# Ten unread matmuls in each batch of the second attention, and four stage hand-overs reordered

## The chip, the cores and the metric

One core of a Trainium2 chip. The metric is the device time of one execution in microseconds; the kernel before has three such times, and one more execution was profiled.

## The reference

Two transformer layers on x of shape (8, 256, 256), each a cross attention and a feed-forward, with a residual around every part and a layer norm without weights ahead of it. All is fp32.

```
x = x + mlstm(norm(x), ctx, ctx)       # 8 heads of 32; decay matrix from gates of q, k, v; RMS norm per head
x = x + bitlinear_ffn(norm(x))         # rows rounded to 8 bits, weights to -1, 0, 1; 256 -> 1024 -> 256, gelu
x = x + linear_attention(norm(x), ctx) # phi(q) phi(k)^T with a causal decay, phi = (elu + 1)^5, over its row sum
x = x + moe(norm(x))                   # 8 experts, the 2 best of each row, 256 -> 1024 -> 256, gelu
```

## The kernel before

Rows lie on partitions: 2048 rows are 16 tiles of 128, two tiles to a batch element. The program is a row of blocks, and in each block every engine has its own written-out instruction list; the engines meet by semaphores inside a block, and all of them at its end.

**Gates (L274 to L467).** VectorE normalizes x in four quarters (`normalize`), TensorE transposes them into `qT` and multiplies windows of the gate weights `Z` with the context (L344) and with the queries (`gates`, L350). Tables of decays follow. `keep_running` (L369) issues unread matmuls: products of the identity whose result nobody reads. Eight of them end this block on TensorE.

**mLSTM and first feed-forward (L542 to L1041), one block.** The mLSTM takes 32 steps n, four to a batch (two row tiles by two head groups). TensorE: `state`, `decay`, `scores`, `values`, `far`; ScalarE: exponentials (L772); VectorE: `product`, `joined`, `denominators`, `square_sums`, `refined`, `scaled`, and `row_stats` of batches that are done; GpSimd splits expert weights into a high and a low bf16 part (L208, L210), adds the residual and takes powers (`row_scales`). Around the loop's end stand the first steps of the feed-forward: `centred` and `first_rounded` (ScalarE), `first_scale` and `first_copied` (VectorE), `first_transposes` and `first_product` (TensorE). Each feed-forward step j works on one tile: `hidden` (L974), gelu and sum of squares (ScalarE), `second_root` and `scaled` (GpSimd), `second_scale`, then the second product. TensorE has 4 + 3 unread matmuls in each step (L627). The ternary weights are made from raw loads by ScalarE (`magnitudes`, `rounded_quarter`, `signs`) during the mLSTM.

**Second attention (L1160 on).** Ten steps j of a software pipeline over the eight batches. TensorE's order in step j:

```
queries(j + 1); scores(j); transposed(j - 1); rank(...); attended(j); logits(j - 1)
```

`queries` transposes the normalized rows (L1427), `scores` is phi(k) phi(q) (L1438, L1440), `transposed` (L1449) and `logits` (L1472) serve the gate of the experts, `attended` is the values product (L1457 to L1459). VectorE masks the scores (`weights`, L1644), divides and adds (`attended`, L1648 to L1652), takes statistics, and in steps 3, 5, 6, 7, 8 and 9 chooses experts (`choose`) and computes the rows' places (`slots`, L1684 to L1688). ScalarE makes exponentials and powers of keys and queries and normed rows. GpSimd takes reciprocal roots (`squared_roots`, L1240), the last product of the keys' powers (`keys`, L1218), low parts of rows, and scatters each tile twice into the experts' lists in HBM (`scatter`, L1234). SP loads keys for batch m + 2 once `keys(m)` is done. Every tile's scatter is placed in GpSimd's list by hand: in step j at 4 or above, one tile before `squared_roots` and one behind it; the tiles of the last two batches come after the loop.

At the end TensorE runs 28 unread matmuls, waits for the last scatters' landing, runs ten more, and waits for the rows of the first block (SP, L1193).

**Experts (L1501 on).** 39 blocks of 128 rows: transposes (L1508), first product (L1546), second product (L1559, L1562), and an accumulating scatter into the sum.

## Time and profile before

| | us |
|---|---|
| median of 3 runs | 614.22 (613.63 to 616.29) |
| the profiled execution, its own time | 610.62 |
| its span, first to last instruction | 608.9 |
| mean granted TensorE clock | 0.908 of full speed |
| TensorE busy | 497.8 (82%) |
| VectorE busy | 399.3 (66%) |
| GpSimd busy | 352.3 (58%) |
| ScalarE busy | 303.2 (50%) |

PE is TensorE, PEld its weight loads, DVE VectorE, ACT ScalarE, POOL GpSimd, SP the sync engine; a name with a q (SPq) is an engine's DMA queue or sequencer. Times in rows are us from the span's start. The granted clock is a share of 2.4 GHz: 1.00 is that level and 0.50 the lower one, 1.2 GHz. Shares of busy time are means over stages with different limits.

### The profile page before, as it was taken

The page shows a single profiled execution, that of the slowest core. Times are in us where ns is not written, and L with a number is a line of the kernel's source. Part 1 is how long each engine was busy: PE and PEld are TensorE (multiplying, and loading weights), DVE is VectorE, ACT ScalarE, POOL GpSimd, SP SyncE. Part 2 cuts the span into 40 slices and gives each one's busy share as a digit, 9 for nine tenths or more (in the row PEclk, how much of TensorE's full clock was granted, in tenths as well). Part 3 has the DMA queues.
Part 4 walks back from the last instruction along what each step waited for, and adds up shares of the span by engine and source line. Part 5 has one row for each costly group of instructions (what it writes and reads, how often), then busy time and mean ns, then how long its engine had stood idle before and what let it go on. Part 6 is the DMA issues. An engine that isn't in the chain of part 4 may idle for free. (4 is left out here: it accounts for less than half of the span.)

```text
span 608.9 us, 13847 instructions
## 1 busy us (share of the span) xinstructions
PE 497.8 (82%) x4467; PEld 365.9 (60%) x4467; DVE 399.3 (66%) x1228; ACT 303.2 (50%) x752; POOL 352.3 (58%) x421
## 2 busy tenths in 40 slices
PE   1979999997688878367666658999999999999960
PEld 1845776663355444246556526788878887888740
DVE  3432678998888888456988635566657676666540
ACT  0234575863789988567764313444344434443410
POOL 3509599782888878524686661445555555455531
PEclk9979999997999999857776678999999999999995
DMA  8733633320132232110142264233223323332225
GB/s 280 120 96 121 209 104 114 105 71 18 36 105 92 83 102 73 38 35 23 56 156 87 79 175 133 42 49 54 48 43 54 53 49 53 45 55 30 26 28 154
DMA packets 50614, 50.14 MB, mean 82 GB/s; under 512 B 21584, under 2 KB 40272, under 8 KB 50384
## 3 DMA queue, kind: packets, MB, share of 16 engines
q1 hardware_dynamic: 41168, 36.04, 20.2%
q0 software_dynamic: 7152, 9.36, 9.7%
q10 hardware_dynamic: 2224, 3.86, 2.0%
q8 instruction: 38, 0.62, 0.4%
q14 instruction: 32, 0.26, 0.2%
HBM read 36.46 MB, written 14.87 MB: 84 GB/s over the span
## 5 line engine op out<-in xcount | busy, mean ns | idle before, releaser
L1394 ACT ACTIVATE region<-cps,aux 128x128 f32<-128x128 f32 x312 | 89.3, 368 | 132.3 <-PE cps L1546 132.3
L1285 POOL CAST vaug<-region 128x512 bf16<-128x512 f32 x78 | 49.1, 630 | 107.9 <-ACT region L1394 96.2
L1546 PE MATMUL cps<-aux,w1hi 128*128 128x128 bf16 x1248 | 109.9, 219 | 0.9 <-DVE aux L1754 0.5
L1546 PE MATMUL cps<-aux,w1lo 128*128 128x128 bf16 x624 | 107.5, 217 | 0.0
L1559 PE MATMUL cps<-w2pair,vaug 128*128 x312 | 105.3, 379 | 0.0
L1546 PEld LDWEIGHTS cps<-aux,w1hi 128*128 x1248 | 95.9, 96 | 5.8 <-DVE aux L1754 0.7
L1562 PE MATMUL cps<-w2pair,vaug 128*128 x312 | 78.7, 273 | 0.0
L1291 POOL DMA_INDIRECT y_sum<-aux x39 | 61.0, 1564 | 15.7 <-issue 6.0
L1546 PEld LDWEIGHTS cps<-aux,w1lo 128*128 x624 | 61.5, 98 | 0.0
L1761 DVE TENSOR_TENSOR vaug<-region,vaug 128x512 bf16<-128x512 f32 x78 | 51.2, 697 | 0.1
L1769 DVE TENSOR_TENSOR aux<-cps,wstage 128x256 f32<-128x256 f32 x39 | 16.6, 425 | 52.7 <-PE cps L1559 51.7
L772 ACT ACTIVATE w2pair<-argp,w2pair 128x128 f32<-128x128 f32 x128 | 36.4, 369 | 24.8 <-PE argp L594 24.5
L1559 PEld LDWEIGHTS cps<-w2pair,vaug 128*128 128x128 bf16 x312 | 30.5, 98 | 28.1
L627 PE MATMUL pvp<-aux,identb 128*128 128x512 bf16 x141 | 39.9, 410 | 0.5 <-DVE w2pair L900 0.5
L1234 POOL DMA_INDIRECT row_buf<-region x32 | 34.1, 1064 | 9.2 <-issue 7.5
L210 POOL TENSOR_TENSOR w1lo<-wstage,w1hi 128x512 bf16<-128x512 f32 x32 | 37.2, 1162 | 2.6
L223 POOL TENSOR_TENSOR w2pair<-wstage,w2pair 128x512 bf16<-128x512 f32 x32 | 36.5, 1160 | 0.4 <-ACT w2pair L216 0.4
L617 PE MATMUL pvp<-vaug,w2pair 128*128 128x33 f32 x256 | 34.8, 281 | 1.0 <-DVE w2pair L888 1.0
L1562 PEld LDWEIGHTS cps<-w2pair,vaug 128*128 128x128 bf16 x312 | 30.5, 98 | 7.5
L617 PEld LDWEIGHTS pvp<-vaug,w2pair 128*128 128x128 f32 x256 | 31.2, 192 | 4.8 <-DVE w2pair L888 1.1
L1754 DVE COPY aux<-cps 128x512 bf16<-128x512 bf16 x39 | 16.5, 424 | 25.6 <-PE cps L1508 25.4
L888 DVE SCALAR_TENSOR_TENSOR w2pair<-scp,w2pair 128x512 f32<-128x512 f32 x32 | 21.9, 686 | 16.0 <-PE scp L605 15.5
(274 smaller groups left out, 1113.2 us busy)
## 6 DMA issues: line engine op xcount, KB each, us to landing
wstage<-in_wall SPq DMA_DIRECT2D x64, 256.0 KB, 2.6
aux<-row_buf SPq DMA_DIRECT2D x39, 129.5 KB, 2.1
x_all<-in_x SPq DMA_DIRECT2D x4, 512.0 KB, 8.9
w2pair<-in_ctxT ACTq DMA_DIRECT2D x2, 1024.0 KB, 11.5
vaug<-in_ctx SPq DMA_DIRECT2D x16, 128.0 KB, 4.0
aux<-in_ctxT SPq DMA_DIRECT2D x8, 256.0 KB, 3.0
y_sum<-x_all SPq DMA_DIRECT2D x8, 256.0 KB, 3.2
w2pair<-in_w1T SPq DMA_DIRECT2D x2, 512.0 KB, 4.7
```

The lines of the kernel that those rows point to most:

```text
L210: pool.tensor_tensor(lo, src, hi, ALU.subtract).then_inc(w_split, 1)
L223: pool.tensor_tensor(w2lo[:, n - E, fs], wstage[:, piece(k)].rearrange("p (f n) -> p f n", n=D), w2hi[:, n - E, fs], ALU.subtract).then_in ...
L617: last = pe.matmul(pvp[:, i, cols], pw[:, n % 2, k, :], vaug[:, TB * b + i, cols], start=True, stop=True)
L627: pe.matmul(unread, identb[:, :], w1q[:, 0, 0:512], start=True, stop=True)
L772: last = act.activation(ew[:, n % 2, k, :], argp[:, BANK[n % NU], k * P:(k + 1) * P], ACT.Exp, bias=bT[:, i, at:at + 1])
L1285: pool.tensor_copy(hhi[:, j % 3, n], hf[:, j % 2, n]).then_inc(hi_done, 1)
L1291: pool.indirect_dma_start(y_sum[:, :], bass.IndirectOffsetOnAxis(ap=y_at[:, i % NA:i % NA + 1], axis=0), ys[:, i % NY], None, compute_op=A ...
L1394: last = act.activation(hf[:, j % 2, f * BLK:(f + 1) * BLK], hp[:, j % 2, f, :], ACT.Gelu, bias=b1T[:, bass.ds(e * NF + f, 1)])
L1546: last = pe.matmul(hp[:, j % 2, f, :], w1(cc * NF + f, part), rowsT[:, j % 2, cc, xpart, :], start=(cc == 0 and n == 0), stop=(cc == NC - ...
L1559: return pe.matmul(yp[:, i % 2, 0:2 * D], hhi[:, i % 3, c0:c0 + P], w2(at, 2), start=(f == 0), stop=(f == NF - 1))
L1562: pe.matmul(yp[:, i % 2, 0:D], hlo[:, i % 3, c0:c0 + P], w2(at, 1), start=False, stop=False)
L1761: dve.tensor_tensor(hlo[:, j % 3, n], hf[:, j % 2, n], hhi[:, j % 3, n], ALU.subtract).then_inc(lo_done, 1)
```

## The change

1. **Gates.** The context part of the gate products becomes `context_gates(half)` and stands behind the transposes of quarters 0 and 1. VectorE makes the gate weights behind the first quarter's statistics. The eight unread matmuls at the block's end go; four stand at the head of the next block's list.
2. **mLSTM to feed-forward.** `centred(0)`, `centred(1)` and `first_scale(0)` move into the last steps of the mLSTM, `first_transposes(0)` ahead of the unread matmuls, of which 8 are left of 16. VectorE's order is `first_scale(1)`, `first_copied(0)` directly behind `joined(7)`; `first_copied(1)` and `row_stats(5)` go behind `hidden(0)`. The row scales are made for tiles 0 to 7, 8 to 11 and 12 to 15, the last two in steps 2 and 4.
3. **Scatters.** A table gives the tiles of each step; one more tile in steps 6 and 7, and two instead of four tiles after the loop.
4. **Second attention.** Ten unread matmuls of 512 columns in each batch, each group behind the wait for its bank and ahead of the wait for its input. At the end 44 and 5 instead of 28 and 10.

```diff
-                    keep_running(8)
...
+                        if q < 2:
+                            context_gates(q)
...
-            SCALED_AT = (0, 4, 12, NT)
+            SCALED_AT = (0, 8, 12, NT)
...
+                    for _ in range(4):
+                        pe.matmul(unread, identb[:, :], flat(heads[:, 0:HG, :]), start=True, stop=True)
                     state(0)
...
-                    pe.wait_ge(pv1_read, B)
-                    keep_running(16)
                     pe.wait_ge(exp_done, UN)
                     pe.wait_ge(o_read, B)
                     first_transposes(0)
+                    pe.wait_ge(pv1_read, B)
+                    keep_running(8)
...
+                        if n >= UN - 3 and n < UN - 1:
+                            centred(n - UN + 3)
-                    centred(0)
-                    centred(1)
-                    centred(2)
+                    first_rounded(0)
                     roots(B - 2)
                     squares(B - 1)
-                    first_rounded(0)
                     first_rounded(1)
+                    centred(2)
                     roots(B - 1)
...
-                        if i < 2:
-                            row_scales(i + 1)
+                        if i in (2, 4):
+                            row_scales(i // 2)
...
+                        if n == UN - 1:
+                            first_scale(0)
                     joined(B - 1)
+                    first_scale(1)
+                    first_copied(0)
+                    denominators(B - 1)
                     refined(B - 2)
                     scaled(B - 2)
-                    denominators(B - 1)
                     square_sums(B - 1)
-                    first_scale(0)
-                    row_stats(B - 3)
-                    first_scale(1)
-                    first_copied(0)
-                    first_copied(1)
                     refined(B - 1)
                     scaled(B - 1)
                     dve.wait_ge(bias_in, 32)
                     for j in range(NT + 2):
                         if j < NT:
                             hidden(j)
-                        if j < 2:
-                            row_stats(B - 2 + j)
+                        if j == 0:
+                            first_copied(1)
                         if j + 2 < NT:
                             first_scale(j + 2)
+                        if j < 3:
+                            row_stats(B - 3 + j)
...
+            SCATTERED = {4: ((0,), (1,)), 5: ((2,), (3,)), 6: ((4,), (5, 6)), 7: ((7,), (8, 9)), 8: ((10,), (11,)), 9: ((12, 13), ())}
...
-                    for b in range(ENDS - 4, B):
-                        scatter(b, 0)
-                        scatter(b, 1)
+                    for i in range(NT - TB, NT):
+                        scatter(i)
...
                     def queries(b):
-                        pe.wait_ge(xc_ready, b + 1)
                         if b:
                             pe.wait_ge(eq_ready, b)
+                        keep_running(5)
+                        pe.wait_ge(xc_ready, b + 1)
...
                     def transposed(b):
-                        pe.wait_ge(xn_ready, b + 1)
                         if b:
                             pe.wait_ge(xt_ready, b)
+                        keep_running(2, 4)
+                        pe.wait_ge(xn_ready, b + 1)
...
                     def attended(b):
-                        pe.wait_ge(w_ready, b + 1)
                         if b:
                             pe.wait_ge(x_done, b)
+                        keep_running(3, 2)
+                        pe.wait_ge(w_ready, b + 1)
...
-                    def keep_running(k):
+                    def keep_running(k, bank=0):
                         for _ in range(k):
-                            pe.matmul(banks[:, 0], identb[:, :], w1hi[:, 0, 0:512], start=True, stop=True)
+                            pe.matmul(banks[:, bank], identb[:, :], w1hi[:, 0, 0:512], start=True, stop=True)
...
-                    keep_running(28)
+                    keep_running(44)
                     pe.wait_ge(moved[(B - 1) % NPK], 16 * 2 * TB * (B // NPK))
-                    keep_running(10)
+                    keep_running(5)
```

## Rows read from the trace of the kernel before

**Rows 1.** Chain that ended last: start us, us, what.
```profile
365.70 4.45 PE cps L1478 x10
```

**Rows 2.** Busy us of each engine by stretch (x instructions), granted clock, DMA.
```profile
137.20:150.20 13.00, 10.48 (x38) 4.84 (x38) 10.21 (x37) 3.87 (x8) 2.56 (x2) 0.74 0.07 21
150.20:250.90 100.70, 78.52 (x463) 45.62 (x463) 81.60 (x217) 81.60 (x124) 82.03 (x101) 0.98 0.23 74
250.90:352.30 101.40, 62.72 (x320) 51.89 (x321) 75.14 (x268) 57.67 (x114) 58.63 (x63) 0.67 0.23 74
```

**Rows 3.** Timeline, gates to mLSTM: start us, us, engine line, [idle before <-releaser].
```profile
9.83 1.40 DVE L409 BATCH_NORM_STATS2 stats<-x_all 128x6 f32<-128x256 f32 x4
...
12.92 9.87 PE L344 MATMUL gp<-w2pair 128*128 128x256 f32 x32 [12.92 <-DMA w2pair<-in_ctxT]
...
13.68 1.38 DVE L402 TENSOR_SCALAR w2pair<-x_all,mv,rstd 128x256 f32<-128x256 f32 x4
...
42.70 3.39 PE L369 MATMUL spare_bank<-w2pair,identb 128*128 128x512 bf16 x8
...
43.35 0.21 DVE L437 COPY w2pair<-tabp 128x64 f32<-128x64 f32 x1
...
46.38 1.76 POOL L813 TENSOR_TENSOR w2pair<-vaug,w2pair 128x256 f32<-128x256 f32 x3 [17.31 <-POOLq L273]
...
47.05 0.72 PE L570 MATMUL argp<-vaug,w2pair 128*128 128x132 f32 x4 [0.96 <-POOL w2pair L813]
...
49.00 1.14 ACT L772 ACTIVATE w2pair<-argp,w2pair 128x128 f32<-128x128 f32 x4 [6.23 <-PE argp L594]
```

**Rows 4.** One stretch of that seam, columns as in rows 2.
```profile
45.00:46.00 1.00, 1.00 (x4) 0.15 (x1) 0.00 (x0) 0.00 (x0) 0.00 (x0) 0.62 0.00 0
```

**Rows 5.** DMA issues of the first microsecond: KB each, us to landing.
```profile
x_all<-in_x SPq DMA_DIRECT2D x1, 512.0 KB, 4.4
```

**Rows 6.** Timeline of VectorE, mLSTM to feed-forward.
```profile
138.66 0.43 DVE L900 TENSOR_TENSOR w2pair<-pvp,w2pair 128x264 f32<-128x264 f32 x1 [0.65 <-PE pvp L617]
...
144.53 0.75 DVE L940 BATCH_NORM_STATS2 stats<-x_all 128x6 f32<-128x256 f32 x2
...
148.60 0.42 DVE L968 TENSOR_SCALAR aux<-argp 128x256 bf16<-128x256 f32 x1 [1.43 <-PE argp L634]
...
150.17 1.28 DVE L974 SCALAR_TENSOR_TENSOR region<-scp,aux 128x1024 f32<-128x1024 f32 x1
```

**Rows 7.** Timeline of TensorE in the second attention.
```profile
285.84 0.71 PE L1457 MATMUL cps<-vaug,aux 128*128 128x264 f32 x2
...
301.21 0.66 PE L1427 MATMUL cps<-ident,aux 128*128 128x128 f32 x4 [3.40 <-DVE aux L1616]
...
317.11 1.25 PE L1457 MATMUL cps<-vaug,aux 128*128 128x264 f32 x2 [0.16 <-DVE aux L1644]
```

**Rows 8.** Timeline of VectorE there: its first operation behind a values product.
```profile
278.62 0.16 DVE L1648 TENSOR_SCALAR aux<-cps 128x2 f32<-128x2 f32 x1 [1.92 <-PE cps L1459]
...
287.48 0.16 DVE L1648 TENSOR_SCALAR aux<-cps 128x2 f32<-128x2 f32 x1 [1.10 <-PE cps L1459]
...
320.15 0.16 DVE L1648 TENSOR_SCALAR aux<-cps 128x2 f32<-128x2 f32 x1 [1.44 <-PE cps L1459]
```

**Rows 9.** Timeline of GpSimd, late attention.
```profile
323.81 1.68 POOL L1234 DMA_INDIRECT row_buf<-region  x1 [0.20 <-issue]
...
348.58 0.99 POOL L1234 DMA_INDIRECT row_buf<-region  x1 [0.16 <-DVE region L1688]
...
362.66 0.96 POOL L1234 DMA_INDIRECT row_buf<-region  x1 [0.30 <-issue]
```

**Rows 10.** Timeline of SP's queue, attention to experts.
```profile
366.46 1.50 SPq L1193 DMA_DIRECT2D aux<-row_buf  x2
```

**Rows 11.** Page, DMA issues: times, KB each, us to landing.
```profile
aux<-row_buf SPq DMA_DIRECT2D x39, 129.5 KB, 2.1
```

**Rows 12.** Line L1234, all its scatters.
```profile
DMA to landing us min/median/max: 2.5/3.0/6.5
```

46 lines of the change are left out of this document (27 added, 19 removed).

## The prediction

> **What bounds the kernel now.** I read the page first, then the chain of waits, the busy table by stretch, the timeline of each place where one stage hands over to the next, and last each engine's timeline through the second attention. The chain covers only the end: the expert stage is TensorE back to back, and what starts it is the last scatter's landing at 365.7 and ten unread matmuls of 4.45 us behind it [rows 1]. Everything ahead of that is latency: in the seam before the first feed-forward (137.2 to 150.2) and in the second attention (250.9 to 352.3) no engine is full, and the granted clock is 0.74 and 0.67 of full speed [rows 2]. So what a seam or the attention saves moves the expert stage one for one, and the expert stage itself is not touched.
>
> The sum is made against the profiled execution (span 608.9, its own time 610.6). The three other runs have the median 614.2, 3.6 above it; I add the change in us to that median.
>
> **Seam 1, gates to mLSTM.** Removed: eight unread matmuls at the end. They run from 42.70 to 46.09, while VectorE's last operation is over at 43.56; the next stage's first operation is GpSimd's at 46.38, 0.29 behind the last matmul [rows 3]. Without them it can start at 43.56 + 0.29 = 43.85: -2.53. Against it: four unread matmuls ahead of state(0). The eight cost 3.39 / 8 = 0.42 each, at the lower clock level (1.2 GHz), which the stretch 45 to 46 shows being left (0.62 [rows 4]). Four cost 1.70, of which 0.67 lies beside GpSimd's first product (46.38 to 47.05 [rows 3]): +1.03. Behind them stand 1.95 us up to the first exponential (47.05 to 49.00), now at full clock; if it is still low there, they take up to twice as long. Bounds 0 and +1.95; I take half, +0.97, since TensorE's work just ahead now has a hole of over a microsecond. Reordered at the start: TensorE begins with transposes, not with the context part of the gates at 12.92. The first quarter of x lands 4.4 us after its issue at 0.8 [rows 5], well ahead of 9.83, where VectorE starts on it, behind the gate weights. Statistics of two quarters lie between 9.83 and normalize(0) at 13.68 [rows 3], 1.92 each; the first now runs before the gate weights. So normalize(0) ends at 13.68 + 1.38 - 1.92 = 13.14 and TensorE starts 0.3 later than before, with the same dense work behind. Seam 1: -2.53 + 1.03 + 0.97 + 0.3 = **-0.2**, bounds -1.2 and +0.8.
>
> **Seam 2, mLSTM to feed-forward.** What sets hidden(0) at 150.17 is VectorE's written-out order: idle 0.65 before joined(7), row_stats(5) from 144.53 (0.75 for its two first operations, some 0.45 for the others), idle 1.43 before first_copied(1) and 0.42 for it [rows 6]. The change fills the first idle time with first_scale(0), lets first_copied(0) come as soon as its transposes are there (these no longer stand behind 16 unread matmuls), and puts first_copied(1) and row_stats(5) behind hidden(0). That is 0.65 + 1.20 + 1.43 + 0.42 = 3.70 less. Late next is refined(7): it waits for ScalarE's two 16-column roots behind square_sums(7), which nothing covers any more; with the smallest operation at 0.16 [rows 8] and the hand-overs I take 0.5, so -3.2. The eight unread matmuls that are left end near 144 and product 0 by 145.7 at the latest, ahead of hidden(0) at 147. centred(0) and (1) now run on ScalarE between exponentials of the last batch; VectorE's last product stands behind row_stats(4) in its own queue, so this is covered, and uncovered costs some 0.9 (two of the size of the 0.42 copy). In the loop one row_stats more stands on VectorE and a smaller power on GpSimd; I count nothing, bounds -0.6 and +1.2. Seam 2: **-3.2**, bounds -3.8 and -1.1.
>
> **The attention's unread matmuls.** Ten in each of eight batches: five before the queries, two before the transposes of the normed rows, three before the values product. The first five stand where TensorE idles, 3.40 us in one batch [rows 7]; cost 0 at either clock, and 2.1 if that hole were gone. The other five lie between the scores product and the values product, where TensorE is often not idle: at half of 0.42 they put up to 1.08 on the path of a batch in which VectorE's weights come at once.
>
> What they can buy: the values product takes 287.48 - 285.84 = 1.64 at full clock and 320.15 - 317.11 = 3.04 at the lower one [rows 7, 8]. The scores, larger, lose as much, so a batch wholly at the lower clock loses some 3 us. Before, the clock changes inside most batches: the 8.86 us from 278.62 to 287.48 [rows 8] are a batch mostly at full clock; the mean of the eight is nearer 10. In three of the slow ones VectorE (the expert choice) is what is late, and neither clock nor fillers matter much. Nor can a batch get far below 9: keys on GpSimd, a load, key exponents, query exponents, normed and key powers form a second loop of that length. So I expect 9.2 where the clock set it: -1.0 in batch 0, -0.8 in 1, +0.35 in 2, -0.45 in 5, nothing in the rest: **-1.9**, with full clock most of the time. Bounds: -4 (fillers all hidden) and +10.7 (rival 1).
>
> **The tail of the attention.** A scatter is 0.96 plus 0.30 issue, 1.26; the last twelve run without a hole from 348.58 to 363.62, and the first waits for VectorE's slots(4) [rows 9]. Two tiles, four scatters, are moved ahead of that point: -5.04. It is paid in part: scatters (6) to (10) come a tile earlier each, and stand before keys(7) and the squared roots of the last two batches, which now come up to a whole tile, 2.5, late, and VectorE's choice and slots with them. GpSimd has holes there, so I take half: +1.3. Fillers at the end: 28 + 10 become 44 + 5. SP's row load is issued at 366.46, 0.8 behind the landing, and takes 2.1 [rows 10, 11]; TensorE was held by its ten matmuls to 370.15, some 1.4 beyond the load. 44 from about 351.7, ten of them at 0.42 and the rest at 0.21, end near 363.2 and five more near 364.3, together with the load: -1.4. The last scatter will share the DMA with the clearing of the tails: landings range from 2.5 to 6.5, median 3.0 [rows 12]: +1.3, between. Tail: -5.04 + 1.3 - 1.4 + 1.3 = **-3.8**, bounds -6.5 and -1.0.
>
> A scatter among VectorE's work took 1.68 instead of 0.96 to 0.99 [rows 9]. The Trainium skill, page "SBUF — State Buffer", section "SBUF: two separate sides", says that VectorE and GpSimd share one port pair under an exclusive lock, where the second fully blocks; by it the scatters moved ahead of the tail meet more of VectorE's work than they did, which speaks for rival 2.
>
> **Sum.** -0.2 - 3.2 - 1.9 - 3.8 = -9.1: 601.5 profiled, 614.2 - 9.1 = **605.1** for the median.
>
> **Rivals.**
> 1. *The clock stays low in the attention and the fillers stand on the path* (slower). Ahead of the values product 3 x 0.42 = 1.26 in seven batches, ahead of the transposes 2 x 0.42 = 0.84 in the four where ScalarE is done in time: 12.2, less 1.5 that VectorE's lateness covers in batches 3 and 6: +10.7. With the other terms (-7.2) that is +3.5: 617.7. For it: the clock fell there before, with TensorE busy 62.7 of 101.4 us. Against it: with such fillers it was 0.98 in the feed-forward [rows 2]. It decides from 0.9 us a batch on.
> 2. *GpSimd becomes the bound*: eight scatters among VectorE's work at 1.68 instead of 0.96, +5.8, slide into squared roots and choice: -3.3, 610.9.
> 3. *Seam 2 is given back* in a feed-forward loop that has its own period, so that the early hidden(0) is worth 1: -6.9, 607.3.
> 4. *Hardly anything to be seen*: rival 1 in half of the batches, about +4 instead of -1.9: 611.
>
> **Chances.** Forecast 0.60, rival 1 0.11, rival 2 0.12, rival 3 0.09, rival 4 0.08. Half a per cent is 3.1 us, about what a measurement of this kernel can tell from no change. Faster (below 611.1): the forecast, rival 3, most of rival 2, half of rival 4: 0.81. Slower (above 617.3): most of rival 1, 0.09. Same: 0.10. The forecast's own range is 601 to 609 (its bounds don't fall together); reaching over rivals 2 to 4 the range is 600 to 612.5, with some 0.05 left below and 0.14 above.
>
> **What would show it.** GpSimd's first product of the mLSTM at 43.9 to 44.2 and the first exponential at 48.0 to 49.5; hidden(0) 3 to 3.6 earlier; a granted clock of 0.85 or more over the attention, with values products of 1.64; the last squared roots about a microsecond late; eight scatters without a hole at the end instead of twelve; expert transposes at about 361. It is wrong if the attention's clock stays near 0.67, or if the expert stage starts less than 5 us earlier.

## Result: 609.07 us after, 614.56 before, ratio 0.9927 (0.9901 to 0.9953)

Four runs of each, 608.94 to 610.22 after and 613.63 to 616.29 before. A second comparison, on another chip, gave 0.9921 (0.9890 to 0.9951). The change gains 4.5 to 5.5 us where the prediction said 9.1. The profiled span is 607.4 (608.9 before), the mean granted clock 0.939 (0.908).

**Where the time went.** I cut both programs at marks that every trace shows, in us. "Changed" are the two executions with the code exactly as changed, "before" the two profiles of the kernel before; the last column is the prediction's. In the other profiles that have these stretches as changed they are 88.4 to 88.8, 10.5, 91.7 to 91.9 and 27.0.

```
stretch                                         before         changed        difference    predicted
start to first exponential                      49.00, 47.44   48.59, 49.27   not told      -0.2
first exponential to last mLSTM product         87.53, 87.57   88.55, 88.80   +1.1          none
last product to hidden(0)                       13.64, 13.61   10.54, 10.53   -3.1          -3.2
hidden(0) to hidden(15)                         89.39, 89.38   91.75, 91.94   +2.5          0
hidden(15) to first attention batch             29.01, 29.02   27.01, 27.01   -2.0          -1.0
first to last attention batch                   71.66, 73.43   72.82, 71.60   -0.3          -0.9 +1.3
last batch to first expert product              31.15, 30.75   30.00, 29.68   -1.1          -5.1
first expert product to the end                 237.5, 238.2   238.1, 237.7   0             0
```

An attention batch is taken at VectorE's first operation behind its values product, the first expert product at the first one with a low part of the weights (w1lo), 0.1 to 0.2 behind TensorE's very first. The first stretch can't be read to a microsecond: over fifteen executions of kernels that have it as changed it was 46.4 to 49.3, over three of the code of before 47.4 to 49.0. From the first exponential on, the two pairs of profiles differ by 1.1 and 4.7.

**Seam 1.** The timeline of the changed kernel (start, duration, instruction, idle time before it and what ended it):

```profile
42.81 0.21 DVE L444 COPY w2pair<-tabp 128x64 f32<-128x64 f32 x1
...
43.56 1.76 POOL L824 TENSOR_TENSOR w2pair<-vaug,w2pair 128x256 f32<-128x256 f32 x3 [16.30 <-POOLq L273]
43.57 1.86 PE L673 MATMUL pvp<-w2pair,identb 128*128 128x512 bf16 x4 [1.33 <-PEq L273]
...
45.23 1.08 PE L577 MATMUL argp<-vaug,w2pair 128*128 128x132 f32 x4
...
48.59 0.62 ACT L783 ACTIVATE w2pair<-argp,w2pair 128x128 f32<-128x128 f32 x2 [6.36 <-PE argp L601]
```

GpSimd's first product starts with the unread matmuls at 43.56 and no longer behind them; TensorE starts the state product when its four are through. First exponential 48.59, before 49.00 [rows 3]: near the forecast, and below what repeats.

The hand-over itself repeats, and so can be read. From VectorE's last copy to the first exponential it is 5.78 or 5.79 in all fifteen profiles that have seam 1 as changed, and 5.65, 5.74 and 5.79 in the three of the code of before (43.35 to 49.00 in [rows 3]). What varies lies ahead of that copy. So GpSimd does start earlier (0.75 behind the copy instead of 3.03), and then the first exponential stands 5.03 behind it instead of 2.62.

**The mLSTM, which the prediction had no term for.** GpSimd and VectorE in its last steps:

```profile
125.04 1.65 POOL L837 TENSOR_TENSOR rr<-aux,mhalf 128x8 f32<-128x8 f32 x1 [0.17 <-DVE aux L959]
...
129.12 1.18 POOL L210 TENSOR_TENSOR w1lo<-wstage,w1hi 128x512 bf16<-128x512 f32 x1
129.31 1.02 DVE L934 SCALAR_TENSOR_TENSOR w2pair<-w2pair 128x16 f32<-128x16 f32 x1
...
130.36 0.69 DVE L899 SCALAR_TENSOR_TENSOR w2pair<-scp,w2pair 128x512 f32<-128x512 f32 x1
130.93 1.15 POOL L210 TENSOR_TENSOR w1lo<-wstage,w1hi 128x512 bf16<-128x512 f32 x1
130.97 1.66 DVE L940 TENSOR_TENSOR w2pair<-w2pair 128x512 f32<-128x512 f32 x1
...
```

GpSimd's power is now of 8 columns, 1.65 instead of 1.02 for 4, and all of GpSimd's later work is that much later. VectorE's operations with two SBUF inputs then wait for it: L934 (0.17 elsewhere) ends with GpSimd's L210, and L940 (0.69 alone) takes 1.66, until 0.55 behind the end of the L210 that began 0.04 ahead of it. L899, which reads PSUM, always takes its 0.67 to 0.69, although in 25 of 32 cases an operation of GpSimd is under way when it starts. This agrees with the Trainium skill, page "SBUF — State Buffer", section "SBUF: two separate sides": a VectorE operation with two SBUF inputs and a GpSimd one that reads SBUF exclude each other for a whole instruction.

**Seam 2.** VectorE ahead of hidden(0):

```profile
144.53 0.74 DVE L926 SCALAR_TENSOR_TENSOR w2pair<-w2pair 128x16 f32<-128x16 f32 x1
145.81 0.81 DVE L932 TENSOR_TENSOR w2pair<-w2pair 128x16 f32<-128x16 f32 x1 [0.53 <-ACT w2pair L727]
...
147.07 0.69 DVE L940 TENSOR_TENSOR w2pair<-w2pair 128x512 f32<-128x512 f32 x1
147.68 1.28 DVE L987 SCALAR_TENSOR_TENSOR region<-scp,aux 128x1024 f32<-128x1024 f32 x1
```

The chain ends as the prediction had it, down to the 0.53 of waiting for ScalarE's roots; hidden(0) stands 10.54 behind the last product, 13.64 before [rows 6].

**The feed-forward loop** gives it back. A lap is 5.68 in the steady part of both kernels. From hidden(0) on they are

```
lap       0    1    2    3    4    5    6    7    8    9    10   11   12   13   14
before    5.90 7.29 6.69 6.08 5.68 5.80 5.57 5.68 5.69 5.68 6.94 5.68 5.68 5.69 5.34
changed   5.87 6.60 6.66 6.65 6.46 6.44 6.77 5.67 5.68 5.67 6.94 5.66 6.05 5.29 5.34
```

GpSimd in some of the changed laps, first operation of a lap (L854) and powers (L837):

```profile
160.10 1.12 POOL L854 TENSOR_SCALAR region<-region,aux 128x1024 f32<-128x1024 f32 x1 [1.65 <-DVE aux L1003]
...
167.84 1.02 POOL L837 TENSOR_TENSOR rr<-aux,mhalf 128x4 f32<-128x4 f32 x1
...
180.16 1.02 POOL L837 TENSOR_TENSOR rr<-aux,mhalf 128x4 f32<-128x4 f32 x1
...
193.08 1.12 POOL L854 TENSOR_SCALAR region<-region,aux 128x1024 f32<-128x1024 f32 x1 [1.99 <-DVE aux L1003]
...
198.75 1.12 POOL L854 TENSOR_SCALAR region<-region,aux 128x1024 f32<-128x1024 f32 x1 [0.72 <-DVE aux L1003]
```

(GpSimd's work on tile i falls into the lap behind hidden(i + 1); the expectations count its laps by tiles.) In a steady lap GpSimd waits 0.72 for VectorE and nothing else; each further wait (1.65, 1.99) and each power (1.02) lengthens the lap. For ScalarE's weights (L216) it waits 0.31 and 0.39 in two of the changed laps, 0.36 in one of before. VectorE's extras are in other laps than GpSimd's:

```profile
155.74 0.75 DVE L953 BATCH_NORM_STATS2 stats<-x_all 128x6 f32<-128x256 f32 x2
...
172.78 0.22 DVE L1002 TENSOR_SCALAR aux<-aux 128x1 f32<-128x1 f32 x1 [1.47 <-POOL aux L848]
...
187.99 0.18 DVE L962 RECIPROCAL aux<-rr 128x4 f32<-128x4 f32 x1
188.32 1.20 DVE L964 TENSOR_SCALAR aux<-rr,aux 128x4 f32<-128x4 f32 x1
```

Row statistics (a third pair now in the loop) make laps 1 and 2 long, where GpSimd waits; the powers lengthen laps 3 and 5, where VectorE waits (1.47 at 172.78); the tables of lap 6, 1.58 with one operation at 1.20, make GpSimd wait again. Before, both kinds fell mostly into laps 1 and 2 and covered each other. In lap 4 TensorE was at the lower clock too (the first product, behind 1.63 of idle time, at 174.88 in 1.58 instead of 1.03), and VectorE waited 0.71 for its transposes. GpSimd's own lap there was 5.67 (173.40 to 179.07), so this can have cost at most the 0.39 by which GpSimd waits for ScalarE in the next.

**The stretches**, to be held against [rows 2] (busy us of PE, PEld, DVE, ACT, POOL, then granted clock, DMA share and GB/s):

```profile
137.15:147.70 10.55, 8.04 (x29) 4.56 (x30) 9.23 (x32) 4.05 (x9) 2.53 (x2) 0.68 0.08 26
147.70:250.75 103.05, 79.47 (x455) 45.99 (x464) 84.70 (x224) 81.33 (x124) 81.22 (x101) 0.97 0.22 72
250.75:351.50 100.75, 67.94 (x393) 46.92 (x402) 74.60 (x268) 56.63 (x114) 60.73 (x67) 0.87 0.24 80
```

The attention's clock is 0.87 instead of 0.67. A values product takes 1.54 at full clock (283.95 to 285.49); batch 5's is still at the lower one, 315.38 to 318.43:

```profile
284.40 0.61 PE L1475 MATMUL cps<-vaug,aux 128*128 128x264 f32 x2
...
315.38 1.25 PE L1474 MATMUL cps<-vaug,aux 128*128 128x264 f32 x2 [0.71 <-DVE aux L1661]
```

**Batches 4 to 7.** From batch 5 to 6 it is 9.93 and 9.95 in the two executions of the changed kernel, but 12.05 to 12.51 in the ten other profiles with the new order of the scatters, and 9.67 to 10.68 in all six with the old order. One operation of VectorE makes the difference. Here it is in the kernel of experiment 6, whose edit lies behind it:

```profile
326.38 2.98 DVE L1704 TENSOR_TENSOR region<-region 128x32 f32<-128x32 f32 x1
326.95 1.28 POOL L1234 TENSOR_TENSOR wstage<-aux 128x512 f32<-128x512 f32 x1
328.18 1.12 POOL L1239 TENSOR_TENSOR region<-wstage,region 128x512 bf16<-128x512 f32 x1
```

The same stretch of the changed kernel:

```profile
326.31 0.19 DVE L1703 TENSOR_TENSOR region<-region 128x32 f32<-128x32 f32 x1
...
327.57 1.29 POOL L1233 TENSOR_TENSOR wstage<-aux 128x512 f32<-128x512 f32 x1
```

An operation of VectorE's slots that takes 0.19 alone takes 2.98, until 0.06 behind the second of GpSimd's two products of the keys. In all ten profiles an operation of the slots does this, in 2.86 to 3.08; in the other eight none of them takes more than 1.5 in this batch. In the changed kernel the slots are made at 326.93, 0.6 before GpSimd's products start. Four of GpSimd's scatters, not two, now stand between its roots and those products, and so put the products beside the slots. How many of the unprofiled executions of the changed kernel meet there isn't known.

**The tail.** VectorE, GpSimd, SP's queue and TensorE of the changed kernel:

```profile
353.56 0.17 DVE L1701 TENSOR_TENSOR region<-cps,aux 128x16 f32<-128x16 f32 x1 [3.02 <-remote]
...
354.67 0.96 POOL L1249 DMA_INDIRECT row_buf<-region  x1 [2.09 <-DVE region L1705]
...
355.53 3.38 SPq L1136 DMA_DIRECT2D row_buf<-region  x3
...
358.46 0.96 POOL L1249 DMA_INDIRECT row_buf<-region  x1 [0.30 <-issue]
...
363.77 1.25 PE L1495 MATMUL cps<-w1hi,identb 128*128 128x512 bf16 x5 [0.41 <-DMA row_buf<-region]
364.88 1.50 SPq L1208 DMA_DIRECT2D aux<-row_buf  x2
...
367.12 0.38 PE L1525 MATMUL cps<-identb,aux 128*128 128x128 bf16 x4 [2.10 <-DMA aux<-row_buf]
...
368.92 0.38 PE L1525 MATMUL cps<-identb,aux 128*128 128x128 bf16 x4 [1.42 <-DMA aux<-row_buf]
...
369.86 0.42 PE L1563 MATMUL cps<-aux,w1hi 128*128 128x128 bf16 x2
```

The last scatter starts 19.2 behind the last batch instead of 22.4 [rows 9]: the 5.04 less the 1.8 by which the scatter that waits for slots(5) comes late. It lands 5.3 behind its start instead of 3.0, and SP's row load stands 6.4 instead of 3.8 behind it [rows 10]. Then TensorE idles 2.10 and 1.42, and part of the first expert block runs at the lower clock (0.42 for two products, 0.28 at full clock).

### The profile page after: what moved, and what is told of

It is laid out like the page before. It is cut to its first block, busy times and chain, and to the rows that moved or that the text cites. A ratio compares the mean times of both kernels' runs of the same rounds, so it can differ in the third digit from the quotient of the medians.

```text
span 607.4 us, 13923 instructions
## 1 busy us (share of the span) xinstructions
PE 499.6 (82%) x4476; PEld 363.2 (60%) x4546; DVE 400.6 (66%) x1228; ACT 301.5 (50%) x752; POOL 349.2 (57%) x421
## 4 chain that ended last, share of the span: by engine, by line
PE 39%; DVE 6%; issue 3%; DMA 3%; ACT 2%; POOL 2%; SPq 1%; another core or an unknown queue 0%; DVEq 0%; POOLq 0%; ACTq 0%
PE cps L1563 18%; PE cps L1576 9%; PE cps L1579 6%; PE cps L1525 1%; DMA y_sum<-aux 1%; DMA aux<-in_ctxT 1%; DVE stats L1617 1%; DVE x_all L1669 1%; DMA row_buf<-region 1%; PE cps L1495 1%; POOL wstage L1233 1%; PE cps L1465 1%; DVE aux L1633 1%; PE cps L1474 1%; PE cps L1476 1%
## 5 line engine op out<-in xcount | busy, mean ns | idle before, releaser
L1563 PE MATMUL cps<-aux,w1hi 128*128 128x128 bf16 x1248 | 111.5, 221 | 0.5 <-DVE aux L1771 0.5
L1563 PE MATMUL cps<-aux,w1lo 128*128 128x128 bf16 x624 | 109.1, 219 | 0.0
L1576 PE MATMUL cps<-w2pair,vaug 128*128 x275 | 93.3, 379 | 0.0
L1579 PE MATMUL cps<-w2pair,vaug 128*128 x312 | 78.7, 273 | 1.9
L783 ACT ACTIVATE w2pair<-argp,w2pair 128x128 f32<-128x128 f32 x128 | 36.4, 368 | 25.2 <-PE argp L601 25.1
L1249 POOL DMA_INDIRECT row_buf<-region x32 | 33.5, 1048 | 12.1 <-issue 7.4
L210 POOL TENSOR_TENSOR w1lo<-wstage,w1hi 128x512 bf16<-128x512 f32 x32 | 37.1, 1160 | 2.6
L1495 PE MATMUL cps<-w1hi,identb 128*128 128x512 bf16 x121 | 34.7, 419 | 3.0 <-ACT aux L1348 1.2
L634 PE MATMUL pvp<-aux,identb 128*128 128x512 bf16 x124 | 35.7, 408 | 0.6 <-issue 0.2
L899 DVE SCALAR_TENSOR_TENSOR w2pair<-scp,w2pair 128x512 f32<-128x512 f32 x32 | 22.0, 687 | 17.6 <-PE scp L612 17.2
```

Of the source, the lines that this page charges most:

```text
L210: pool.tensor_tensor(lo, src, hi, ALU.subtract).then_inc(w_split, 1)
L783: last = act.activation(ew[:, n % 2, k, :], argp[:, BANK[n % NU], k * P:(k + 1) * P], ACT.Exp, bias=bT[:, i, at:at + 1])
L1495: pe.matmul(banks[:, bank], identb[:, :], w1hi[:, 0, 0:512], start=True, stop=True)
L1563: last = pe.matmul(hp[:, j % 2, f, :], w1(cc * NF + f, part), rowsT[:, j % 2, cc, xpart, :], start=(cc == 0 and n == 0), stop=(cc == NC - ...
L1576: return pe.matmul(yp[:, i % 2, 0:2 * D], hhi[:, i % 3, c0:c0 + P], w2(at, 2), start=(f == 0), stop=(f == NF - 1))
L1579: pe.matmul(yp[:, i % 2, 0:D], hlo[:, i % 3, c0:c0 + P], w2(at, 1), start=False, stop=False)
```

## Experiments

Ratios are to the kernel before on the same chip, with their intervals; distances are from the profiled execution. Each kernel is the changed one with the edit shown, unless said otherwise.

**1. No unread matmuls in the attention.**

```diff
-                        keep_running(5)
-                        keep_running(2, 4)
-                        keep_running(3, 2)
```

> The changed kernel without the ten unread matmuls of each attention batch, all else as changed. Theory (they raise the clock and so shorten the batches; worth about what the wait of VectorE for the values product gained by batch 6, 2.5 us, less what the last batches gave back): granted clock over the attention falls from 0.87 to about 0.67, values products of the first batches go back from 1.8 to about 3, the attention ends 1.5 to 2.5 us later, ratio to the kernel before 0.9955 to 0.997. Rival (the fillers cost on the path what the clock gives, and the attention's gain is only the seams' shift): time within 0.5 us of the changed kernel, ratio 0.9925. A third (they cost more than they give): ratio below 0.991.

Ratio 1.0028 (1.0011 to 1.0046): slower than the kernel before, some 6 us slower than the changed one. Clock over the attention 0.64:

```profile
249.10:359.50 110.40, 67.38 (x325) 55.37 (x326) 77.87 (x268) 57.55 (x114) 64.00 (x68) 0.64 0.22 75
```

First batch 29.0 behind hidden(15), as before; first to last batch 78.4 against 71.6 and 72.8. No expectation had so much. Batches 4 to 7 alone take 37.4, in the kernel before, equally without unread matmuls, 33.2 and 34.9: the new order of the scatters costs there (batch 5 to 6 is 12.50, with one operation of the slots at 2.97).

**2. Scatters and last unread matmuls as before.**

```diff
-SCATTERED = {4: ((0,), (1,)), 5: ((2,), (3,)), 6: ((4,), (5, 6)), 7: ((7,), (8, 9)), 8: ((10,), (11,)), 9: ((12, 13), ())}
+SCATTERED = {4: ((0,), (1,)), 5: ((2,), (3,)), 6: ((4,), (5,)), 7: ((6,), (7,)), 8: ((8,), (9,)), 9: ((10,), (11,))}
-                    for i in range(NT - TB, NT):
+                    for i in range(NT - 2 * TB, NT):
-keep_running(44) ... keep_running(5)
+keep_running(28) ... keep_running(10)
```

> The changed kernel with the scatters in the order of the kernel before and 28 + 10 unread matmuls at the end. Theory (the last scatter's start gains 4.2, of which a slower landing of the last rows, 5.3 instead of 3.0 behind the last start, and a cold first expert block take back 2.5 to 3): the last scatter starts about 4 us later than in the changed kernel, lands 3 us behind it, the span is 1.5 to 2 us longer (609), ratio 0.9955. Rival (the moved scatters are worth their full price): span 4 us longer, ratio above 0.999. Rival (all of it is given back at the landing): ratio 0.9925 to 0.993.

Ratio 0.9948 (0.9927 to 0.9970), close to the 0.9955 expected: the new tail is worth 1.3 to 1.7 us by the middle values, and the intervals overlap, so that this gain isn't shown. Batches 4 to 7 take 33.0 here, 33.6 and 34.9 in the changed kernel. The distance from last scatter to row load was not the expected one: 6.1, with slots(5) 6.7 behind the choice.

**3. and 4. GpSimd's powers regrouped.**

```diff
-SCALED_AT = (0, 8, 12, NT)
-                        if i in (2, 4):
+SCALED_AT = (0, 4, 12, NT)                # 3: powers behind tiles 0 and 2
+                        if i in (0, 2):
+SCALED_AT = (0, 4, 10, NT)                # 4: one ahead of residual(B - 2), one behind tile 2
+                        if i == 2:
```

> The changed kernel with GpSimd's powers regrouped: 4 columns ahead of the loop instead of 8, 8 columns in lap 0 of the feed-forward loop and 4 in lap 2, where VectorE's laps are long too (row statistics, tables). Theory (an extra of VectorE and one of GpSimd in different laps add up, in one lap they cover each other; and the 4 columns more in the mLSTM, 0.63 us, make all of GpSimd's later operations there that much late and VectorE with them): the last mLSTM product starts 0.6 earlier (136.5), hidden(7) at 191 instead of 193.1, the span 1.5 to 2.5 us shorter. Rival (the laps 0 to 6 are bound by VectorE and the clock alone): hidden(7) stays within 0.5 of 193.1, and only the 0.6 of the mLSTM may show. Rival (something absolute, the loads of the expert weights, holds the loop at 193): no change at hidden(7) even with hidden(0) earlier.

> The changed kernel with GpSimd's powers as 4 columns in the mLSTM, 6 in its idle stretch after the last mLSTM batch (137 to 144), and 6 in lap 2 of the loop. GpSimd then has one extra of some 1.3 us in the loop instead of two of 1.02, VectorE its tables in laps 2 and 8. Theory (GpSimd's lap of 5.68 is the bound of the loop and each extra that is not covered adds): the last product 0.6 earlier, hidden(7) at 190 to 191.5, span 1.5 to 3 us shorter. Rival (the laps are VectorE's and the clock's): gain of at most the 0.6.

Ratios 0.9892 (0.9860 to 0.9924) and 0.9892 (0.9859 to 0.9926), spans 606.8 and 606.5. First exponential to last product is back at 87.91 and 87.53: the 8 columns cost 0.6 to 1.3. The loop gained less than the theory said: hidden(0) to hidden(7) 45.20 and 45.08, against 45.45. Lap 2 grew to 8.15 and 8.62, where VectorE now makes tables (1.20 for one operation beside GpSimd) and row statistics in one lap. So regrouping GpSimd alone isn't it; VectorE's own sum in a lap counts, which theory and rival had each half. Against the changed kernel's 0.9921 on the same chip both are some 1.8 us faster by the middle values, within the intervals.

**5. The two seams alone** (edits of 1 and 2 together).

> The changed kernel without the attention's unread matmuls, with the scatters in the order of before and 28 + 10 unread matmuls at the end: so the two seams alone. Theory (the loop gives the seam's 3.1 us back, save some tenths): from the first exponential on the attention starts within 0.7 us of the kernel before, ratio 0.998 to 1.001. Rival (the two seams keep about 2.5 us and the attention's parts lose it): ratio 0.9945 to 0.9965. The batches of the attention take 71 to 73 us from the first to the last read of a values product if the late batches' 78.4 of the run without unread matmuls came from the new order of the scatters, and 78 if it did not.

Ratio 1.0021 (1.0002 to 1.0040), 1.3 us slower than before. First exponential to hidden(15) is 190.8 against 190.6: seam 2's 3.1 is gone in mLSTM and loop. From first to last batch 73.1, so the 5.3 more of experiment 1 (78.4) came from the scatters' order. The tail is 2.8 to 3.2 longer than before, though it is the same code: slots(5) stands 7.2 behind the choice.

Both runs without unread matmuls show one thing more. Batches 1 to 4 take 30.8 in experiments 1 and 5, at a granted clock of 0.67, and 28.4 in both profiles of the kernel before, at 0.82, although in experiment 5 the attention has the instructions of the kernel before, with only two neighbouring waits of TensorE exchanged in three places. TensorE is busy 22.6 and 22.5 instead of 19.7 with the same 96 operations. So the seams also cost 2.4 there, through the clock; why it differs is open. That is a reason why the ten unread matmuls don't have one price: beside the seams they gain 4.5 us (experiment 2 against this one), on the kernel before 2.8 (experiment 11).

**6. A probe of that wait.**

```diff
+                        if j == ENDS - 1:
+                            for _ in range(6):
+                                chain(dve.tensor_scalar(spare_row, low, 1.0, None, ALU.mult))
                         if j in chosen_in:
                             slots(chosen_in[j])
```

> The changed kernel with six chained operations of 8 columns on VectorE between the choice and the slots of the last batch, where its trace shows VectorE idle for 3.0 us although TensorE's ranks are there after 1.0. Theory A (VectorE gets its instructions late there): the six also start late or the gap moves with the instruction count, and the slots come 1.2 us later or at another distance. Theory B (only the wait on TensorE's ranks ends late): the six run at once at 350.5, 0.2 each, the slots start unchanged about 3.0 us after the choice's last operation. Theory C (nothing but the queue in front): slots start at the end of the six, 1.3 us after.

```profile
352.15 0.18 DVE L1697 TENSOR_TENSOR region<-region 128x2 f32<-128x2 f32 x1
352.25 1.44 DVE L1732 TENSOR_SCALAR aux<-aux 128x8 f32<-128x8 f32 x6
355.43 0.17 DVE L1702 TENSOR_TENSOR region<-cps,region 128x16 f32<-128x16 f32 x1 [1.73 <-remote]
```

The six ran at once, and the slots still came 3.1 behind the choice: theory B. One profile and a single time of 611.4.

**7. Unread matmuls up to the expert stage.**

```diff
-                    keep_running(5)
+                    keep_running(14)
+                    keep_running(7)
                     transposes(1)
```

> The changed kernel with 14 instead of 5 unread matmuls behind the landing and 7 between the transposes of the first two blocks, so that TensorE has no hole of 2.1 and 1.4 us before the expert stage. Theory (the first expert block ran at the lower clock from 369.9 to 373 because of these holes, 1.2 to 1.5 us): transposes at the same distance behind the row load, first block at 0.17 a triple of products instead of 0.31, span 1 to 1.5 us shorter, ratio 0.990 to 0.991. Rival (the lower clock there comes from something else, or the matmuls stand in the way of the row load's first transposes): the same or slower by up to 1.

Ratio 0.9943 (0.9916 to 0.9970), not faster. SP's queue and TensorE:

```profile
365.49 1.50 SPq L1208 DMA_DIRECT2D aux<-row_buf  x2
...
367.63 0.38 PE L1525 MATMUL cps<-identb,aux 128*128 128x128 bf16 x4 [0.39 <-DMA aux<-row_buf]
369.32 1.68 PE L1495 MATMUL cps<-w1hi,identb 128*128 128x512 bf16 x7 [1.31 <-issue]
370.84 0.39 PE L1525 MATMUL cps<-identb,aux 128*128 128x128 bf16 x4
```

The seven begin 1.3 behind the first transposes (TensorE's list works out block 0's weight addresses in between) and hold the second transposes to 370.84. From first expert product to the end it is 237.1 instead of 238.1 and 237.7, the gain of a warm start, but the first product comes 5.7 behind the row load instead of 4.4 and 4.6. The rival holds.

**8. The changed kernel again.**

> The changed kernel as it is, a second profile and time on the chip that the other three of this call use. Theory: ratio 0.991 to 0.994 as before; from the first exponential to the last mLSTM product 88.6, product to first hidden 10.5, first to last hidden 91.8, VectorE's wait for the ranks 3.0 again. Rival (the 88.6 and the 3.0 were chance of one execution): 87.5, or a wait of 1.0.

Ratio 0.9921 (0.9890 to 0.9951), span 606.5, slots 2.98 behind the choice; 88.80, 10.53, 91.94. The code decides them, not chance.

**9. The last unread matmuls held until the slots are made.**

```diff
                     pe.wait_ge(eq_ready, B)
+                    pe.wait_ge(slot_ready, len(GROUPS))
-                    keep_running(44)
+                    keep_running(40)
```

> The changed kernel with the unread matmuls behind the last ranks (40 of them) held until VectorE has made the last slots. Every run with the seams changed shows VectorE's last slots 3.0 to 7.2 us after the choice, though the ranks are recorded as done after 1.05. Theory (the semaphore of the ranks is only seen once some unread matmuls behind them are through): the slots start 1.05 after the choice's last operation, everything behind (clears, row load) 2 us earlier, span 1.5 to 2 us shorter, ratio 0.989 to 0.991. Rival (the wait has nothing to do with them): the gap stays 3.0 and the time is that of the changed kernel or up to 0.5 longer.

Ratio 0.9948 (0.9920 to 0.9976). The slots come 1.04 behind the choice, but nothing is won by it:

```profile
350.93 0.17 DVE L1702 TENSOR_TENSOR region<-cps,aux 128x16 f32<-128x16 f32 x1 [1.04 <-issue]
...
352.90 3.92 SPq L1136 DMA_DIRECT2D row_buf<-region  x4
...
356.05 0.96 POOL L1249 DMA_INDIRECT row_buf<-region  x1 [0.30 <-issue]
...
363.36 1.50 SPq L1208 DMA_DIRECT2D aux<-row_buf  x2
```

From the first clear on SP's queue to the row load it is 10.5 now, 9.35 and 8.4 in the two executions of the changed kernel. Columns below as in the stretches above; the mean busy share of the DMA engines is the last but one:

```profile
355.00:357.00 2.00, 2.00 (x6) 0.63 (x5) 1.26 (x6) 0.00 (x0) 1.70 (x2) 0.50 1.14 255
357.00:359.00 2.00, 2.00 (x10) 0.93 (x9) 0.00 (x0) 1.49 (x2) 0.01 (x1) 0.97 1.06 197
```

The 16 DMA engines are full from 355 to 359 with the clears of the tails and the last scatters. In the changed kernel's second execution they were at 0.94 and 1.00 from 357.5 to 361.5. In the kernel before they were as full, 0.99 from 355 to 363, but its last scatter started only at 362.66 and landed 3.0 later. GpSimd's scatters are no longer what the tail waits for.

**10. The kernel before again, and 11. the kernel before with the ten unread matmuls.**

```diff
+                        keep_running(5)       # queries, behind the wait for eq_ready
+                        keep_running(2, 4)    # transposed, behind the wait for xt_ready
+                        keep_running(3, 2)    # attended, behind the wait for x_done
```

> The kernel before, unchanged, a second profile and a measure of what the comparison calls no change. Expected: ratio 0.998 to 1.002; first exponential anywhere between 46.6 and 49.3, from it to the last mLSTM product 87.5, first to last hidden 89.4, first to last attention batch 71.7. If the wait for the last ranks is 1.0 again, its absence in the kernel before is a property of the program, if 3 or 7, it is chance. If the batches take 73 as in the run of the seams alone, the 71.7 was chance.

> The kernel before with the attention's ten unread matmuls a batch and nothing else. Theory (they are what makes the changed kernel faster, by the clock: undoing them cost 6.5 us, adding them to the two seams alone gained 4.5): 3.5 to 5.5 us faster, ratio 0.991 to 0.9945. Rival (they only repair what the new scatters cost; the 1.9 us of the prediction is their price on the kernel before): ratio 0.996 to 0.998.

The first: 1.0001 (0.9976 to 1.0026), slots 1.04 behind the choice, laps as before. First to last batch 73.43 against 71.66: that stretch varies by two microseconds from execution to execution. The second: 0.9954 (0.9930 to 0.9979), 2.8 us faster, less than the theory's 3.5 to 5.5 and more than the rival's. Its first batch is 26.99 behind hidden(15), slots 1.04.

**12. VectorE's extras moved** (with GpSimd's powers as in 4, the last behind tile 1).

```diff
+                    row_stats(B - 3)          # ahead of refined(B - 1)
+                    tables(slice(4, 10))      # the same, behind a wait for rr_ready
-                        if j < 3:
-                            row_stats(B - 3 + j)
+                        if j < 2:
+                            row_stats(B - 2 + j)
+                        if i == 6:            # in second_scale, ahead of its wait for root_ready
+                            tables(slice(10, NT))
```

> The changed kernel with VectorE's extras out of the critical stretch of the feed-forward laps: row statistics 5 and the tables of tiles 4 to 9 stand between the last square sums and the refinement that waits for ScalarE's roots, row statistics 6 and 7 in laps 0 and 1, the tables of tiles 10 to 15 inside second_scale of lap 6, where VectorE waits for GpSimd's root; GpSimd's powers as 4 columns in the mLSTM, 6 in its idle stretch and 6 in lap 1. Theory (in the loop every microsecond by which VectorE holds GpSimd up is lost, since GpSimd's own 5.68 a lap is the bound): first hidden 1 to 1.5 us later than in the run with 4, 6 and 6 columns alone (10.5 behind the last product becomes 11.5 to 12), first to last hidden 87 to 88.5 instead of 91.4, span 2 to 3 us shorter, ratio 0.985 to 0.9875. Rival (the laps are held by the weight loads or ScalarE): first to last hidden stays above 90.5.

Ratio 0.9891 (0.9850 to 0.9931), span 604.9. Hidden(0) comes 11.2 behind the last product, hidden(15) 87.8 behind hidden(0), 4.0 less than in the changed kernel; 1.2 of that is lap 10 (5.70 instead of 6.94), which was long in the kernel before too. GpSimd's power behind tile 1 falls into lap 2, where VectorE waits for it; from there on GpSimd waits the steady 0.72, save for 1.08 and 0.81 in two laps:

```profile
160.31 1.36 POOL L837 TENSOR_TENSOR rr<-aux,mhalf 128x6 f32<-128x6 f32 x1
...
165.59 0.21 DVE L1005 TENSOR_SCALAR aux<-aux 128x1 f32<-128x1 f32 x1 [1.82 <-POOL aux L848]
...
166.21 1.12 POOL L854 TENSOR_SCALAR region<-region,aux 128x1024 f32<-128x1024 f32 x1 [0.72 <-ACT w2pair L216]
...
```

The tables inside lap 6 cost 0.1 (5.77), where they had cost 1.1. So the laps are GpSimd's, and whatever keeps it waiting is lost; the rival (loads, ScalarE) falls. In the whole kernel's time the gain doesn't show yet: the ratio missed the 0.985 to 0.9875 expected and is that of experiments 3 and 4. The slots came 1.01 behind the choice here, though TensorE's list is that of the changed kernel. The attention took 2 us more than elsewhere from batch 0 to 1 (12.5, at a granted clock of 0.73; 10.2 at 1.00 in experiment 13), and 12.1 from batch 5 to 6, with the operation of the slots at 3.08.

**13. to 16. On top of 12**: the hold of 9; that with the attention's unread matmuls doubled; that with only the five ahead of the queries; and 12 with the scatters' old order, without the hold.

> The kernel with VectorE's and GpSimd's extras moved, as in the run of that name, and the last unread matmuls (40) held until the last slots are made. Theory (the transfers of clears and last scatters, full from 2 us behind the first clear on, set the row load): as without the hold, within 0.3 per cent; gap of the slots 1.0; row load 24.3 to 24.8 behind the last attention batch. Rival (the hold gains 1 us or more by itself): ratio 0.3 per cent lower or more.

> The same with the attention's unread matmuls doubled: ten ahead of the queries, four and six later. Theory A (some batches are still long because the clock falls in them; more activity holds it up): batches 0 to 1 and 5 to 6, 12.1 to 12.5 in some runs and 10.0 to 10.3 in others, come down to the short values, the time is 1 to 3 us shorter. Theory B (the later ones stand on the path; ten more a batch at 0.21 each are 1.0 us for the five more ahead of the values and transposes): 4 to 8 us longer.

> The same with only the five unread matmuls ahead of the queries. Theory A (those five hold the clock, the other five cost up to 0.2 each on the path): the same time or up to 3 us shorter. Theory B (the other five are what keeps TensorE active between scores and values): the clock over the attention falls to 0.7 to 0.8, values products of 3 us in some batches, 2 to 5 us longer.

> The extras moved, the unread matmuls of the attention as changed, no hold, but the scatters in the order of the kernel before (44 + 5 unread matmuls at the end as changed). Theory (the new order gives its 5 us back in the late batches, 2 to 3, and at the transfers, 2): within 1.5 us of e12's run, up to 1.5 longer; batches 4 to 7 33 us instead of 34.3 to 36, last scatter 22.5 behind the last batch instead of 17.5 to 19. Rival (the prediction's: worth 3.8): 3 us or more longer.

```
run                       ratio (interval)            batch to batch
13 moved, slots first     0.9857 (0.9821 to 0.9892)   10.23  8.73 10.63  9.51 11.41 12.05  9.98
14 doubled                0.9942 (0.9921 to 0.9963)   10.93  9.39 10.35  9.40 13.72 12.05 11.41
15 five only              0.9878 (0.9845 to 0.9912)   10.45  8.71 10.58  8.95 14.62 12.05  9.21
16 old order              0.9903 (0.9870 to 0.9936)   10.29  8.73 10.16  9.65 11.40 10.17 10.84
```

Doubling costs 5 us. Batches 0 and 1 are 0.70 and 0.66 longer, although the clock is full from 260 to 310: theory B, and at most the first half of its price. Without the five behind the queries the middle value is 1.3 us higher, within the intervals, so the first five may do nearly all of it; no run of this list has neither. The old order is within them too (0.9903 against 0.9857): against 13 its batches are 1.3 shorter from first to last, its tail 1.9 longer. Against 12, from which it differs in nothing else, the row load stands 25.1 behind the last batch instead of 24.3, and the DMA engines are full for 6 us in both (0.99 from 347 to 353, 1.01 from 353 to 359): the last rows land 2.4 behind the last scatter's start here, 6.0 in 12, and the four scatters saved are worth 0.8. Number 13, 601.7 us against 610.3, is the fastest kernel of the study; on another chip 9's hold alone had won nothing that the intervals show, and how much of the 0.9857 is the hold isn't settled (its row load stands 23.2 behind the last batch, below the 24.3 to 24.8 expected).

## Why the prediction was half right

**Direction and range** held, 609.1 in 600 to 612.5. The size failed.

**Seam 1** (-0.2): the hand-over, for which the sum had -2.53 + 1.03 + 0.97 = -0.53, is worth nothing: 5.78 instead of 5.65 to 5.79. GpSimd's start came 2.3 earlier, but what follows it grew by 2.4, not by 2.0. The +0.3 for the new start can't be read.

**Seam 2** (-3.2): the term itself measured -3.1. The step that failed is the one behind it: "In the loop one row_stats more stands on VectorE and a smaller power on GpSimd; I count nothing, bounds -0.6 and +1.2." The loop took +2.5, outside the bounds, because each power in GpSimd's list and each wait of GpSimd for VectorE's extras adds to its lap of 5.68, and the larger first power +1.1 in the mLSTM, for which there was no term although the diff shows it. The two seams together made the kernel 1.3 us slower (experiment 5), not 3.4 faster, with the attention's 2.4 and a longer tail on top. Rival 3, held at 0.09, named the place; its mechanism was another. The loop's period isn't a wall that an early start runs into: GpSimd's 5.68 has no slack, and each delay is lost whether the start is early or not. Experiment 12 shows it: it starts 0.7 later than the changed kernel and ends 3.3 earlier.

**The attention** (-1.9): on the kernel before -2.8 (-4.3 to -1.3), right in kind and near in size. The clock rose to 0.87 as said, experiment 15 gives no sign that the other five cost anything, and rival 1 did not come true, though experiment 14 shows that its price is real from the double number on. Missed was batch 0, -2.0 instead of -1.0, and that the parts don't add: beside the seams the same ten are worth 4.5 us, beside the new order of the scatters as well 6.

**The tail** (-3.8): -1.1 behind the last batch. The -5.04 was there in the order of GpSimd's work, but the +1.3 for the landing was too small: from the last scatter's start to the row load it is +2.1 to +2.6, and slots(5) came 2.0 late on top. That it is the DMA engines' own time for clears and scatters agrees with their full share in experiments 9, 12 and 16; no run takes the clears away. Removing that lateness moved the row load by 0.3 to 0.9 against the last batch (experiment 9). The late batches (4 to 7) pay more than the 1.3 forecast: without unread matmuls 37.4 instead of 33.2 and 34.9, with them 33.6 to 37.1 in five executions of the changed order (the changed kernel and 6, 7, 8, 9) against 33.0, 31.2 and 32.4 in 2, 11 and 16. Some 2 of this are the slots' operation that waits for GpSimd's products, in ten of the twelve profiles with the new order. Rival 2, held at 0.12, named the two engines; it looked for the loss in longer scatters. The prediction's own sign of being wrong came true: the expert stage starts less than 5 us earlier (row load 364.88 instead of 366.46 [rows 10], first expert transposes 367.12, not 361).

**What stays open** is why slots(5) waits. In nine profiles of nine kernels or executions with the changed lists of VectorE it stood 2.9 to 7.2 behind the choice, in all three of the code of before 1.04, in 12 to 16 at 1.00 to 1.04. VectorE was able to work (experiment 6). Holding the unread matmuls back removed it (9), but so did other lists of VectorE and GpSimd with the unread matmuls in place (12, 16). The traces name no releaser of this program's engines. The seams' list brought it in, at a price of about 3 us in experiment 5 and under 1 in the changed kernel.

## What to carry to other kernels

In a loop whose lap one engine fills, read from the trace which wait of that engine is the last, and price every operation put in front of it at its full length; an extra of the other engine was free here only in a lap in which the first has one too, or in a place where it waits anyway. Work moved out of a seam into the laps behind it isn't gone: sum both, and look at sizes changed in the same edit, such as a power of 8 columns for one of 4. And when a list of descriptor-issuing instructions is shortened, ask what the transfers themselves take; behind the queue stood the DMA engines. An operation moved in time also moves against the other engines: look at what it now runs beside, in more than one profile, since a race can go either way.

## What had not been expected of the hardware

- VectorE's short operations on SBUF stretch to the end of a GpSimd operation that began just ahead: 0.17 to 1.02, 0.69 to 1.66, 0.24 to 1.20, beside GpSimd operations of 1.12 to 1.18. One that begins just ahead of two products of GpSimd waits for both, 2.86 to 3.08 instead of 0.17 to 0.19.
- The same code reaches the first exponential between 46.4 and 49.3 us after its first instruction, so a difference of profiled spans says little below 3 us, and distances between marks say more.
- So a batch of the attention has two lengths in executions of the same instructions (batch 5 to 6: 9.93 and 9.95 in the two of the changed kernel, 12.50 in the runs of experiments 6 and 7, whose edits lie behind it). Batch 0 to 1 has two as well, and there it is the clock: 10.2 at 1.00 in experiment 13, 12.1 at 0.86 in 11 and 12.5 at 0.73 in 12.
